# The second layer norm of blocks 0 to 6, moved from the feed-forward into the mixer of the next block

## The reference

```
h = layernorm(x) * (1 + ca) + sa
x = x + ga * mixer(h)          # mixer: q, k, v = rms(h) @ wqkv; running sums of exp(k)*v and exp(k);
                               #        y = sigmoid(q) * ratio; h + (u * silu(g)) @ wout
h = layernorm(x) * (1 + cb) + sb      # the second norm
x = x + gb * ffn(h)            # ffn: 4-bit weights, silu(gate) * up, down, then divided by its rms
```

## Time and profile before

| | us |
|---|---|
| median of 3 runs | 2038.09 (2038.05 to 2041.14) |
| span of the profiled execution | 2036.9 |
| mixer iterations 1 to 5, each | 162.0 to 162.1 |
| feed-forward, from 1401.47 | blocks of 75.4 to 78.3, the last 72.95 |

### The profile page before, as it was taken

The page is one execution under the profiler, slowest core; times in us unless marked ns, Lnnn a source line. Parts: engine busy times, 40 slices in busy tenths (PEclk is TensorE's granted clock), DMA queues, the critical chain, the costliest instruction groups (busy, mean ns, idle before and its releaser), DMA issues. The chain is left out here.

```text
span 2036.9 us, 25294 instructions
## 1 busy us (share of the span) xinstructions
PE 1888.6 (93%) x8376; PEld 826.3 (41%) x8376; DVE 1382.7 (68%) x1795; ACT 921.8 (45%) x1421; POOL 959.1 (47%) x680
## 2 busy tenths in 40 slices
PE   4638999999999999999999999998999999999996
PEld 1213444444444444444444444443443433433432
DVE  6996884884874866777678457245657768768756
ACT  4445334333423433523432421122776776776773
POOL 0553422421522521431441231213889889989974
PEclk7869999999999999999999999998999999999998
DMA  8223012012012012101101101313101011011011
GB/s 308 83 68 95 24 35 81 11 39 93 5 40 95 6 35 67 40 26 54 62 26 37 60 6 47 112 35 127 63 1 63 22 42 63 22 42 62 0 42 62
DMA packets 62147, 112.06 MB, mean 55 GB/s; under 512 B 4464, under 2 KB 20848, under 8 KB 61424
## 3 DMA queue, kind: packets, MB, share of 16 engines
q1 hardware_dynamic: 62064, 111.06, 16.3%
HBM read 80.11 MB, written 30.93 MB: 55 GB/s over the span
## 5 line engine op out<-in xcount | busy, mean ns | idle before, releaser
L532 PE MATMUL bank<-Y,wsw 128*128 128x512 f16 x3072 | 684.0, 379 | 8.7 <-DVE late L843 8.4
L786 POOL TENSOR_TENSOR late<-late 128x512 f16<-128x512 f32 x128 | 192.1, 1501 | 633.1 <-ACT late L661 633.0
L532 PEld LDWEIGHTS bank<-Y,wsw 128*128 128x128 f16 x3072 | 299.0, 98 | 376.6 <-DVE late L843 12.0
L1621 DVE SCALAR_TENSOR_TENSOR f_A<-bank,gu_s,f_A 128x512 f32<-128x512 f32 x352 | 260.7, 741 | 177.8 <-ACT f_A L1445 166.8
L509 PE MATMUL bank<-late,wout 128*128 128x512 f16 x1536 | 352.4, 379 | 3.6 <-POOL late L786 3.5
L1445 ACT ACTIVATE f_A<-bank,gu_s 128x512 f32<-128x512 f32 x352 | 241.6, 687 | 157.6 <-PE bank L1370 139.1
L487 PE MATMUL bank<-H,wqkv 128*128 128x512 f16 x1152 | 260.1, 387 | 37.0 <-DVE H L868 30.9
L1525 POOL TENSOR_TENSOR f_A<-f_A 128x512 f32<-128x512 f32 x176 | 253.9, 1443 | 72.9 <-DVE f_A L1621 72.4
L1335 PE MATMUL bank<-f_HH,f_down_hi 128*128 128x512 f16 x704 | 267.3, 382 | 20.2 <-POOL f_HH L1535 19.7
L843 DVE TENSOR_TENSOR late<-late,bank 128x512 f32<-128x512 f32 x128 | 87.7, 685 | 227.4 <-PE bank L532 206.8
L653 ACT ACTIVATE late<-bank 128x512 f32<-128x512 f32 x128 | 76.4, 597 | 350.1 <-PE bank L532 265.5
(11 more groups left out here) (151 smaller groups left out, 2143.8 us busy)
## 6 DMA issues: line engine op xcount, KB each, us to landing
room<-packed SPq DMA_DIRECT2D x48, 176.0 KB, 2.4
X<-xT SPq DMA_DIRECT2D x8, 1024.0 KB, 6.0
h_scratch<-X SPq DMA_DIRECT2D x8, 1024.0 KB, 4.2
f_X<-x_scratch SPq DMA_DIRECT2D x8, 1024.0 KB, 5.5
f_N<-x_scratch SPq DMA_DIRECT2D x7, 1024.0 KB, 5.5
outT<-f_X SPq DMA_DIRECT2D x7, 1024.0 KB, 4.2
late<-xT SPq DMA_DIRECT2D x24, 256.0 KB, 2.9
HR<-h_scratch SPq DMA_DIRECT2D x24, 256.0 KB, 3.2
```

Of the source, the lines that this page charges most:

```text
L532: mm = nc.tensor.matmul(out[:], wsw[:, pw, k, col:col + P], Y[:, px, k, :], start=(k == 0 and pw == 0 and px == 0), stop=(k == DT - 1 and ...
L786: nc.gpsimd.tensor_tensor(UG[:, j % 2, 1, :], G, UG[:, j % 2, 0, :], ALU.subtract).then_inc(UG_low, 1)
L1621: nc.vector.scalar_tensor_tensor(a, EV[ev_bank(j, m)][:], gu_s[:, which * I_T + j, g:g + 1], a, ALU.mult, ALU.add).then_inc(by_dve, 1)
```

## The change

The second norm of blocks 0 to 6 is taken out of the feed-forward (and out of the mixer's last iteration for block 0) and put into the mixer's next iteration. Block 7 keeps it in the feed-forward, beside block 6.

- The residual of block b works in a new buffer `X2` of four tiles. x comes with one DMA, h tile by tile into two buffers during `swiglu(b)`; DVE adds ga*h in steps 9, 10, 14 and 15 (`residual_h`), and ga*out after the last step (`residual`, from the four banks). The four x1 tiles are stored from `X2`.
- In iteration b+1, `n_adds` and `n_add_squares` (GpSimd), `n_reduce` after groups 5 and 11 of `qkv` (TensorE, bank 2), `n_centre` (DVE), `n_squares` after the seventh copy and `n_sqrt` between the roots of q and k (ACT), `n_scale` (DVE: one reciprocal, four scalings) ahead of `inverse(KSQ)`. The halves are made by `n_split` (ACT) and `n_lower` (DVE) in steps 2 and 4 and stored to `h2_dram` (SyncE). `decode_chunk(b, 0)` moves from behind `hidden(b, 0)` to the front of the iteration.
- The last iteration does the same for block 6 in its steps; it loads the halves of block 0 into `H`.
- In the feed-forward, blocks 0 to 5 have no norm beside them. SyncE loads `H[s]` from `h2_dram` for blocks 1 to 6. Three banks are used in steps 2 to 5 only in block 6, in step 4 in the other blocks with a previous one, and nowhere in block 0.

```diff
@@ sync @@
+            def load_x2(b):
+                ...
+                sp.dma_start(X2[:], xT_t[:, :, tok(b)]).then_inc(x2_loaded, 16)
+            def load_h(b, c):
+                ...
+                sp.dma_start(HT[c % 2], h_t[:, c, tok(b)]).then_inc(res_loaded[c % 2], 16)
+            def store_n(b, c):
+                sp.wait_ge(n_low, lows)
+                sp.dma_start(h2_dram[...], HS[:, c % 2, :, :]).then_inc(n_stored[c % 2], 16)
                 store_values(b, 0)
                 load_words(b, 2)
+                if not start and not last:
+                    for c in range(DT):
+                        store_n(b - 1, c)
+                if not last:
+                    load_x2(b)
+                    load_h(b, 0)
+                    load_h(b, 1)
                 store_values(b, 1)
@@ tensor @@
                         n += 1
+                        if not (isinstance(b, int) and b <= 1) and n in (5, 11):
+                            n_reduce(b - 2, n == 11)
@@ scalar @@
+                    if n == 2 * DT - 2 and not (isinstance(b, int) and b == 1):
+                        n_squares(b - 2)
...
                     sqrt(QSQ, b + 1)
+                    if not (isinstance(b, int) and b == 0):
+                        n_sqrt(b - 1)
                     sqrt(KSQ, b + 1)
                 for j in range(FT):
                     silu(b, j)
...
+                    if s2 and j in (2, 4) and not (isinstance(b, int) and b == 0):
+                        n_split(b - 1, j - 2)
+                        n_split(b - 1, j - 1)
@@ gpsimd @@
+                if norm:
+                    n_adds(b - 1)
                 if s2:
                     add_squares(QSQ, b + 1)
+                    if norm:
+                        n_add_squares(b - 1)
@@ vector @@
+            def residual_h(b, c):
+                dve.wait_ge(x2_loaded, 16 * (b + 1))
+                dve.wait_ge(res_loaded[c % 2], 8 * DT * b + 16 * (c // 2 + 1))
+                nc.vector.scalar_tensor_tensor(X2[:, c, :], HT[c % 2], mod[:, GA][:, c:c + 1], X2[:, c, :],
+                                               ALU.mult, ALU.add).then_inc(res_sum, 1)
+            def n_scale(b):
+                dve.wait_ge(n_root, b + 1)
+                nc.vector.reciprocal(RS2[:], RS2[:]).then_inc(n_recip, 1)
+                ...
+                for c in range(DT):
+                    nc.vector.scalar_tensor_tensor(X2[:, c, :], X2[:, c, :], mod[:, CB][:, c:c + 1], RS2[:],
+                                                   ALU.mult, ALU.mult).then_inc(n_scaled, 1)
+                if s2 and norm:
+                    decode_chunk(b, 0)
+                    n_centre(b - 1)
+                    n_scale(b - 1)
                 if s2:
                     inverse(KSQ, b + 1)
                 for j in range(FT):
                     hidden(b, j)
+                    if s2 and norm and j in (2, 4):
+                        n_lower(b - 1, j - 2)
+                        n_lower(b - 1, j - 1)
+                    if s2 and j in (9, 10, 14, 15):
+                        residual_h(b, (9, 10, 14, 15).index(j))
@@ feed-forward @@
-            iteration(0, 0, False, True)
-            iteration(1, 1, True, True)
-            iteration(2, 0, True, True)
-            with eng.Fori(3, NB - 2, 2) as b:
-                iteration(b, 1, True, True)
-                iteration(b + 1, 0, True, True)
+            iteration(0, 0, False, False)
+            iteration(1, 1, True, False)
+            with eng.Fori(2, NB - 2, 2) as b:
+                iteration(b, 0, True, False)
+                iteration(b + 1, 1, True, False)
+            iteration(NB - 2, 0, True, True)
             iteration(NB - 1, 1, True, False)
-        R_STEPS = range(2, 6)
+        def r_steps(prev, nxt):
+            return range(2, 6) if nxt else range(4, 5) if prev else range(0)
```

More of the change, by code:

```diff
@@ L379, in iteration @@
             def iteration(b, s1):
+                start = isinstance(b, int) and b == 0
+                last = isinstance(b, int) and b == NB - 1
                 load_words(b, 0)
@@ L396, in iteration @@
                 for k in range(2, CHUNKS):
+                    if not last and k == CHUNKS - 2:
+                        load_h(b, 2)
+                        load_h(b, 3)
                     store_values(b, k)
@@ L399, in iteration @@
                         load_words(b, k + 2)
-                    if not s1 and b == NB - 1 and k == GU_CHUNKS - 1:
+                    if last and k == GU_CHUNKS - 1:
                         sp.wait_ge(qkv_done, QKV * NB)
@@ L404, in iteration @@
                         sp.dma_start(v["values"], v["gu_dram"]).then_inc(values_loaded, 16)
[L405 to L410, removed]
+                        for half in n_stored:
+                            sp.wait_ge(half, 8 * DT)
+                        sp.dma_start(H[:], h2_dram[:, 0]).then_inc(H_loaded, 16)
+                if not last:
+                    store_x1(b)
             iteration(0, True)
@@ L447, in bank_read, with n_reduce @@
                     pe.wait_ge(root[FAMILY[kind]], 2 * b)
+                    if kind == MEAN and not (isinstance(b, int) and b <= 2):
+                        pe.wait_ge(n_root, b - 2)
+            def n_reduce(b, squares):
+                if squares:
+                    pe.wait_ge(n_sq_sum, 3 * (b + 1))
+                    pe.wait_ge(n_centred, DT * (b + 1))
+                else:
+                    pe.wait_ge(n_sum, 3 * (b + 1))
+                    pe.wait_ge(root[0], 2 * NB if isinstance(b, int) and b == NB - 2 else 2 * (b + 3))
+                nc.tensor.matmul(N_BANK[:], ones[:], RS2[:], start=True, stop=True).then_inc(n_var if squares else n_mean, 1)
             def reduce_tiles(kind, b):
@@ L1457, in beside @@
             def beside(b, s, place, prev, nxt):
-                for there, n, start, work in ((prev, b - 1, COPY_Y, copy_y), (nxt, b + 1, SQUARE_N, square_n),
-                                              (prev, b - 1, SQUARE_Y, square_y)):
-                    due, c = now(place, start)
-                    if there and due:
-                        work(n, c)
+                due, c = now(place, COPY_Y)
+                if prev and due:
+                    copy_y(b - 1, c)
+                due, c = now(place, SQUARE_N)
+                if nxt and due:
+                    square_n(c)
+                due, c = now(place, SQUARE_Y)
+                if prev and due:
+                    square_y(b - 1, c)
                 due, c = now(place, HIGH_N)
@@ L1481, in iteration @@
                                 high(b - 1, I_T - 1)
[L1482 removed]
+                        take(b, j, m, steps)
                     silu(b, j)
@@ L1538, in beside @@
             def beside(b, place, prev, nxt):
-                for there, n, start, work in ((nxt, b + 1, ADD_X, add_x), (nxt, b + 1, ADD_N, add_n),
-                                              (prev, b - 1, ADD_Y, add_y)):
-                    due, c = now(place, start, 2)
-                    if there and due and c < NSUM:
-                        work(n, c)
+                due, c = now(place, ADD_X, 2)
+                if nxt and due and c < NSUM:
+                    add_x(c)
+                due, c = now(place, ADD_N, 2)
+                if nxt and due and c < NSUM:
+                    add_n(c)
+                due, c = now(place, ADD_Y, 2)
+                if prev and due and c < NSUM:
+                    add_y(b - 1, c)
             def iteration(b, s, prev, nxt):
@@ L1630, in beside @@
             def beside(b, s, place, prev, nxt):
-                for there, n, start, work in ((nxt, b + 1, CENTRE, centre), (nxt, b + 1, INVERT_N, invert_n),
-                                              (nxt, b + 1, SCALE_N, scale_n), (prev, b - 1, INVERT_Y, invert_y),
-                                              (prev, b - 1, NORM_Y, norm_y), (prev, b - 1, RESULT, result)):
+                for start, work in ((CENTRE, centre), (INVERT_N, invert_n), (SCALE_N, scale_n)):
                     due, c = now(place, start)
-                    if there and due:
-                        work(n, c)
+                    if nxt and due:
+                        work(c)
+                for start, work in ((INVERT_Y, invert_y), (NORM_Y, norm_y), (RESULT, result)):
+                    due, c = now(place, start)
+                    if prev and due:
+                        work(b - 1, c)
                 if first(b) and place < 2 * DT:
```

388 lines of the change are left out of this document (220 added, 168 removed).

## The result

The changed kernel takes 2056.84 us (median; 2055.66 to 2057.61), the kernel before 2039.18 on the same chip. The ratio is 1.0084, with a 95% interval from 1.007 to 1.0098: slower by 17.7 us, where 2048.5 was forecast. The profiled execution has a span of 2054.1 us, against 2036.9. The feed-forward starts at 1452.39 instead of 1401.47 (+50.9 us for all that comes before) and takes 601.7 us instead of 635.4 (-33.7).

The account below looks back on a forecast made before the run. The prediction took the mixer to be bound by TensorE: 7.1 us per iteration times six gave +43 us, the feed-forward -32. With 10.5 us added to the 2038 median it forecast 2048.5 us, range 2033 to 2063.

Parts of the forecast that it names:

- Two sums, 1.72: Mixer's q/k/v part: two new sums by a matrix of ones on TensorE add 1.72 us per iteration, with nothing hiding them.
- Wait for the product of step 0, 5.3: Mixer, from swiglu's start S: the gate product starts at S+12.4 behind norm work on DVE; TensorE waits 5.3 us per iteration.
- Scalings at 2.7, not the upper price: Mixer, DVE: four scalings take 2.7 us together because GpSimd is idle, instead of 3.9 beside GpSimd's work.
- Vanished wait, -1.6: Mixer, step 1: chunk 0 no longer stands between two gate products, so TensorE's 1.51 us wait goes; 1.6 with handover.
- Clock, 1.7 with bounds 0 and 3.4: Mixer, behind the new wait: TensorE's lowered clock adds 1.7 us per iteration; 0 if not lowered, 3.4 if low twice as long.
- "Nothing, bound +1" for steps 2 to 5: Mixer's later steps: low halves make DVE 1 to 3 us late, within 4.4 allowed; no cost, bound +1 us per iteration.
- A cover for everything in the q/k/v part: Mixer's q/k/v part: chunk 0's unpacking, centring and ACT's squares fit behind the matmuls and cost nothing.
- Feed-forward -32: Feed-forward: blocks 1 to 5 gain 22 us together, block 0 9, block 7 1; sum -32 us, bounds 25 and 47.
- Rival 1: Mixer: the clock is not lowered by the new wait, or only in some iterations; 2039, or 2044 for half; chance 0.17.
- Rival 2: Feed-forward: only the boundary's waits remain, blocks 1 to 5 take 69.4 us instead of 72.0; 2034 or 2029; chance 0.18.
- Rival 3: Mixer stalls more, by late squares before k's eviction or late steps 2 to 5: 10 us an iteration, 2068; chance 0.12.
- Rival 4: Mixer: norm's root is ready before the last eviction and scalings hide in the q/k/v part; mixer +10, 2016; chance 0.03.

Follow-up runs that it names:

- first experiment: Against the changed kernel, the norm's reciprocal moved behind the scaling of k in step 0, its four scalings behind the reciprocal of step 1; 2040.28 us, ratio 1.0008.
- third experiment: Against the changed kernel, the second pair of low halves (split on ACT, subtraction on DVE) moved from step 4 to step 5; 2051.72 us, ratio 1.0053.

## Why the prediction was right, and where its terms were off

The sign, the place and the mechanism were right; 2056.84 lies in the range and 8.3 us above the forecast. On the span the forecast was 2048 and 2054.1 was measured: the first part lost 50.9 us instead of 43, the feed-forward gained 33.7 instead of 32. Term by term:

- *Two sums, 1.72.* Measured 1.72.
- *Wait for the product of step 0, 5.3.* The product was forecast for S+12.4 and stood at S+12.2 (694.47, S = 682.24). The wait is 4.57 longer than before; 0.64 of the rest was taken by the root of k. Together 5.2. The run with the scalings in step 1 confirms their part, 2.93 of it with the handover.
- *Scalings at 2.7, not the upper price.* Measured 2.74, beside an idle GpSimd. The rule of contention by the Trainium skill (GPSIMD Engine Reference, Key points) did not act there. Where GpSimd works beside such operations the traces agree, and they show either engine paying. In the first experiment GpSimd's `low` takes 4.01 us instead of 1.16, while DVE's four products take 2.49. In the changed kernel the same four products take 6.68 us (709.18), beside a `low` of 1.60 and GpSimd's own products behind it; in the kernel before it was 4.53 and 1.48.
- *Vanished wait, -1.6.* Measured -1.67.
- *Clock, 1.7 with bounds 0 and 3.4.* Measured 1.4 to 1.6; over the runs from 1.3 to about 3.0, within the bounds. That this term came so close is partly luck, since the kernel of the third experiment, with the same waits, paid up to twice as much.
- *"Nothing, bound +1" for steps 2 to 5.* **This step failed**: 1.83 in step 4. The prediction asked how late DVE might come. It didn't ask what the two `n_split` do to ACT, whose squares lead through GpSimd to a sum. In the kernel before, GpSimd's additions (3.87 us beside the scan) had 2.5 us to spare: two copies of 0.7 us on ACT don't fill that, but with what came late in steps 2 and 3 they did.
- *A cover for everything in the q/k/v part.* Right for the evictions. The prediction had seen that the root of k moves to third place and costed only DVE's reciprocal from it, not the bank that it frees: 0.64.
- The terms of the mixer sum to 8.6 instead of 7.1 in iterations 1 to 5, 7.5 us together: this is the first part's gap of 8.
- *Feed-forward -32.* Measured -33.7: blocks 1 to 5 at 70.8 to 72.2 (72.0 forecast), block 0 at 68.12 (69.4; 66.43 to 68.12 over the runs). The nearest row, the last block, carried this. The fourth bank, put at 1.0, is 0.7. ACT loses nine operations a block and not eight, the root with them.

Rival 1 (the clock holds) is refuted for a wait of 4.4 us: the clock fell in every one of these iterations. Its other half has something to it: how long it stays low changes from one iteration to the next, and at block 4's start a wait of 2.35 us lowered it in one kernel and one of 2.47 us didn't in another. This agrees with the page TensorE: Matmul & The Clock Gate, What's actually happening, of the Trainium skill, which says that the monitor runs freely and doesn't start with the kernel. Rival 2 (the feed-forward runs free, under 70) is refuted as a forecast of the changed kernel; with the boundary's wait removed 70.2 was reached, near its 69.4. Rival 3 named the right weakness, late steps 2 to 5, and overpriced it. Rival 4 needed the norm's root before the last eviction, and it came at 684.07, after it.

## What to carry to other kernels

Work that is moved beside an engine at its limit costs by its place: here the same instructions gave +51 us or +1 (feed-forward from 1452.39 or from 1402.49), by whether a root, a reciprocal, four scalings and the making of the halves stood ahead of something that TensorE wanted soon. For each engine that receives moved work, follow what is queued behind it to the next thing that the bound engine waits for, ACT and the banks that its reads free included. The nearest row of the trace (the block that already lacks the work) priced the gain to 2 us of 34.

## What the runs showed of the hardware

- **The clock's price for the same wait varies.** After 4.41 us of idle TensorE, 12 matmuls took 3.91 to 5.09 us in iterations of one kernel (third experiment), where 2.59 is the full pace. In the worst of them the next 12 still ran slowly at first (695.59, 2.90 us). Two kernels with the same mixer code differed by 0.9 us in one iteration by this alone. Differences of 1 us per iteration between kernels with such waits can't be laid to their edits.
- **Waits of nearly one length go both ways.** The granted clock fell behind a wait of 2.35 us (block 4 with the early result) and stayed up behind one of 2.47 us (the same place with the mixer's edits added). Behind 2.68 us in the first experiment it was low at once in one iteration (the two sums took 2.07 us); in another the sums ran at full clock, 1.12 us, and it fell only behind the wait of 0.92 us that follows. It didn't fall behind 1.48 us, nor behind 2.05 us. The changed kernel by stretch, TensorE alone, behind the wait that ended at 695.22 (span, busy, granted clock):

```profile
695.00:696.00 1.00, 0.78 (x2) 0.50 0.00 0
...
697.00:698.00 1.00, 1.00 (x4) 0.50 0.00 0
698.00:699.00 1.00, 1.00 (x5) 0.90 0.00 0
```

- **A hardware loop's second turn** made DVE late in both kernels in which nothing else was late there: its first `f_A` came 5.15 and 5.28 us after the block's start instead of 1.44, TensorE waited 2.35 and 2.47 us, and the block took 74.40 and 72.98 us instead of 70.2. In the changed kernel it is hidden by the wait at the boundary: block 4 takes 72.23 us, block 3 72.03.
- **DVE and GpSimd slow each other, and either can pay.** The same four products on DVE took 2.49, 4.53 and 6.68 us in three kernels, and the `low` on GpSimd that met them 4.01, 1.48 and 1.60 us. A row's time for such an operation is to be taken over only with what stood beside it on the other engine.
